# Last half's gates kept early in SBUF, its logits made from turned x2, its tile stores issued behind the logits

## The chip, the cores and the metric

The kernel runs on one core of one Trainium2 chip. The metric is device time in microseconds (us), the median of several executions. All data is fp32.

## The reference, cut to what matters

```
x = x + mamba(cond(x))            # D_INNER 512, 16 states, forward + reversed direction, in_proj/out_proj
x2 = x @ w_bot[b].T + bias        # per batch, 256 -> 256
# mixture of experts on x2, added to x2, the result added to x:
logits = x2 @ Wg + bg             # 256 -> 8
topv, topi = top_k(logits, 2);  w = softmax(topv)
xs = x2[:, :, None, :] * w[..., None]
out = x2
for e in range(8):
    h = silu(xs @ W1[e]) * (xs @ W3[e]);  y = h @ W2[e]
    out = out + where(topi == e, y, 0).sum(2)
result = x + out
# inside each direction of mamba:
x, z = split(h @ in_proj_w.T);  x = silu(conv(x));  ...;  y = scan(...) * silu(z)   # silu(z): the gates
return y @ out_proj_w.T
```

x is 2 batches of 1024 tokens by 256 channels. The gates multiply the sum of the forward and the reversed scan, since both directions share z.

## The kernel before, in words

The work has two big stages and a short one between them.

**The scan loop.** One program for each engine, each with the same loop over NU = 256 items. An item `i` is (q, th, pr, n): q is batch times direction (4 of them, 64 items each, `at(q, s)` is item 64q + s), th which half of the 512-token halves, pr which pair of the four 128-channel blocks, n the state. For an item ScalarE makes two decays (`decay`), VectorE does a product, two scans (`u`, `scans`) and, for every fourth item, one more product (`own_product`), GpSimd does the other products, and TensorE adds the result into two PSUM banks `Y[0]`, `Y[1]` by multiplying with the identity (`add`, two matmuls of 128x512). Sixteen items make one pair of blocks of one half; `evac` (ScalarE) then copies `Y` into `ya` in SBUF.

**Side work in the loop.** All else is hung on items by hand-written tables: `STEP_AT` (step widths; a matmul with 16 rows), `GATE_AT` (the gates z: two matmuls of 128x512, then Silu on ScalarE in place in PSUM, then `gated` on VectorE, the product with `ya`), `OUT_AT` (out projection, `out_block`), `TILE_AT` (a tile is 128 tokens: `tile` makes x2 and the turned x, `tile_T` turns x2 back to channels by tokens, `tile_lg` makes the logits, `tile_top` on VectorE takes the top two). TensorE runs a table's step in `side_work(i)` ahead of `add(i - 2)`; the other engines a few items later. Side work takes one of two PSUM banks (numbers 6 and 7, `both_side`); `take` waits until the bank's last user has freed it.

**Between the stages.** For the last half (batch 1, tokens 0 to 511, written (1, 0)) gates 0 and 1 stand at items 60 and 62 of q = 3, gates 2 and 3 after the loop; then `gated`, `out_block`, four `tile`, four `tile_T`, four `tile_lg`, one after the other on TensorE. The x2 and x rows of a tile are stored to DRAM by SyncE (`store`). VectorE then computes the routing: which of 39 (NT) tiles of 128 token slots belongs to which expert, in some 50 small steps that wait for each other by name (`after`, semaphore `dv_rt`): `mm` (the one-hot sum), a pair of 128x128 matmuls on it (L511, L512), `eid` (the expert of each tile), `hit`, `hot`. TensorE then multiplies 32 times 128x78 (L519, "the token lists" here) to invert the permutation. `warm(n)` is n matmuls of 128x512 into a bank that nobody reads, six behind `eid` and four behind the token lists.

**The expert stage.** 39 tiles: a gather of 128 tokens (GpSimd, `fetch`), W1, W3 and W2 of the expert loaded by SyncE (`load_13`, three buffers, 3 x 1 MB), matmuls L545 and L556, and an indirect DMA that adds to the output. The weights' buffers lie in the arena that the scan loop used.

## Time and profile before

| | us |
|---|---|
| median of 3 runs (1439.96, 1444.07, 1444.72) | 1444.07 |
| the profiled execution | 1444.52 |
| its span, first to last instruction | 1442.6 |
| scan loop, first scan to the last product of VectorE | 49.04 to 952.2 |
| between the stages, to the first expert matmul | 952.2 to 1010.91 |
| expert stage, 39 tiles | 1010.91 to 1442.6 |

All times below are from the span's start. A row of the timeline gives start, duration, engine, line, what is written from what, how many instructions, and in brackets the idle time before it and what ended it. An fp32 matmul is two instructions. Where rows of one engine overlap by some 0.1 us, the ends are modelled. The clock column gives TensorE's granted clock as a share of full speed: 1.00 is 2.4 GHz, 0.50 is 1.2 GHz.

### The profile page before, as it was taken

Reading aid. Unit: us, or ns where it says so; the run is one execution under the profiler, and the core shown is the slowest. Engines: PE = TensorE matmul, PEld = TensorE weight load, DVE = VectorE, ACT = ScalarE, POOL = GpSimd, SP = SyncE. Lnnn points to the kernel's source line nnn. Section 1 sums busy time; section 2 is a strip of 40 time slices with the busy share of each in tenths; the row PEclk is TensorE's granted clock in tenths of the full one; section 3 lists DMA queues with packets and bytes.
Section 4 is the critical chain, followed back from the end, with each engine's and each line's share of the span. In section 5 each row is a group of like instructions: output and inputs, shape, how many; then the busy total and the mean of one; then the engine's idle time right before and its main releaser. Section 6 shows DMA issues by size and latency. Waiting matters only on the chain.

```text
span 1442.6 us, 16563 instructions
## 1 busy us (share of the span) xinstructions
PE 1317.4 (91%) x5278; PEld 785.1 (54%) x5278; DVE 959.1 (66%) x1155; ACT 705.5 (49%) x1251; POOL 994.7 (69%) x519
## 2 busy tenths in 40 slices
PE   7999989899998978898888978897999999999997
PEld 3343333343333423333333434445999999999996
DVE  3798999999999999979999999955111111111110
ACT  3787775686786585766656564430211111111111
POOL 1799999999999999989999999931222222222211
PEclk9999999999998999979999999996999999999999
DMA  4645445445454445435554544514898898898892
GB/s 170 182 148 165 141 153 150 146 146 160 138 166 158 152 144 167 146 117 167 172 157 156 180 162 154 177 54 182 299 323 305 320 321 305 317 330 301 323 320 57
DMA packets 103193, 282.46 MB, mean 196 GB/s; under 512 B 9265, under 2 KB 19122, under 8 KB 87618
## 3 DMA queue, kind: packets, MB, share of 16 engines
q1 hardware_dynamic: 95618, 271.17, 54.6%
q0 software_dynamic: 7488, 10.23, 3.3%
q8 instruction: 43, 0.70, 0.2%
q14 instruction: 44, 0.36, 0.1%
HBM read 271.40 MB, written 9.96 MB: 195 GB/s over the span
## 4 chain that ended last, share of the span: by engine, by line
PE 32%; DMA 13%; POOL 5%; DVE 1%; SPq 1%; issue 1%; POOLq 0%; ACT 0%; DVEq 0%
DMA arena<-bc_scratch 12%; PE ps_y L545 10%; PE ps L556 9%; PE ps_du L545 5%; PE ps_u L545 5%; POOL arena L1083 3%; POOL arena L1079 1%; SPq L1169 1%; PE ps_de L519 1%; PE ps_de L531 1%; POOL arena L1051 0%; PE ps_y L414 0%; POOL arena L1069 0%; DMA out_x<-arena 0%; PE ps_du L361 0%
## 5 line engine op out<-in xcount | busy, mean ns | idle before, releaser
L414 PE MATMUL ps_y<-arena,ident 128*128 128x512 f32 x1024 | 510.2, 630 | 83.8 <-POOL arena L1083 82.6
L1083 POOL TENSOR_TENSOR arena<-arena 128x1024 f32<-128x1024 f32 x192 | 455.1, 2380 | 14.3 <-DVE arena L845 7.6
L414 PEld LDWEIGHTS ps_y<-arena,ident 128*128 128x128 f32 x1024 | 192.6, 197 | 364.0 <-issue 213.9
L658 ACT ACTIVATE ps_de<-arena,An 128x512 f32<-128x512 f32 x256 | 176.4, 689 | 264.6 <-DVE arena L842 263.7
L1069 POOL TENSOR_TENSOR arena<-arena 128x1024 f32<-128x1024 f32 x128 | 301.8, 2358 | 5.2 <-issue 3.6
L1121 POOL DMA_INDIRECT out_x<-arena x39 | 61.8, 1585 | 317.2 <-ACT arena L784 308.6
L829 DVE TENSOR_TENSOR ps_u<-ps_du,arena 128x512 f32<-128x512 f32 x256 | 178.6, 698 | 23.9 <-DVE arena L856 8.9
L658 ACT ACTIVATE arena<-arena,An 128x512 f32<-128x512 f32 x256 | 181.0, 707 | 0.0
L1034 DVE TENSOR_TENSOR arena<-ps_du,arena 128x512 f32<-128x512 f32 x39 | 27.0, 692 | 231.2 <-PE ps_du L545 231.2
L842 DVE TENSOR_TENSOR_SCAN arena<-ps_de,hlast,arena 128x512 f32<-128x512 f32 x128 | 163.0, 1274 | 0.3
L842 DVE TENSOR_TENSOR_SCAN arena<-ps_de,arena 128x512 f32<-128x512 f32 x128 | 155.3, 1213 | 4.8 <-ACT arena L658 2.4
L545 PE MATMUL ps_y<-arena 128*128 128x128 f32 x1248 | 152.1, 275 | 0.5 <-ACT arena L772 0.5
L545 PEld LDWEIGHTS ps_y<-arena 128*128 128x128 f32 x1248 | 148.4, 192 | 2.6 <-ACT arena L772 0.7
L556 PE MATMUL ps<-arena 128*128 128x256 f32 x624 | 141.2, 379 | 0.5 <-issue 0.5
L556 PEld LDWEIGHTS ps<-arena 128*128 128x128 f32 x624 | 115.6, 190 | 15.0 <-issue 0.9
L845 DVE TENSOR_TENSOR_SCAN arena<-arena,hlast,ps_u 128x512 f32<-128x512 f32 x96 | 120.5, 1255 | 0.0
L845 DVE TENSOR_TENSOR_SCAN arena<-arena,ps_u 128x512 f32<-128x512 f32 x96 | 114.6, 1194 | 0.0
L325 PE MATMUL ps<-arena 128*128 128x512 f32 x224 | 107.4, 602 | 0.0
L1034 DVE TENSOR_TENSOR arena<-ps_u,arena 128x512 f32<-128x512 f32 x39 | 27.0, 692 | 120.7 <-PE ps_u L545 120.7
L784 ACT ACTIVATE arena<-ps 128x256 f32<-128x256 f32 x39 | 14.9, 383 | 180.4 <-PE ps L556 171.1
L778 ACT ACTIVATE arena<-ps_y 128x512 f32<-128x512 f32 x78 | 46.6, 597 | 112.0 <-PE ps_y L545 112.0
L1079 POOL TENSOR_TENSOR arena<-arena 128x512 f32<-128x512 f32 x64 | 82.7, 1293 | 4.4 <-PE ps_y L414 4.4
(216 smaller groups left out, 1515.2 us busy)
## 6 DMA issues: line engine op xcount, KB each, us to landing
arena<-bc_scratch SPq DMA_DIRECT2D x256, 512.0 KB, 4.6
arena<-in_W SPq DMA_DIRECT2D x117, 1024.0 KB, 8.0
arena<-in_xT SPq DMA_DIRECT2D x2, 1024.0 KB, 5.5
arena<-in_w2c SPq DMA_DIRECT2D x1, 2048.0 KB, 8.3
arena<-in_xT SPq DMA_DIRECT2D x4, 512.0 KB, 6.2
X_scratch<-stg SPq DMA_DIRECT2D x12, 128.0 KB, 4.7
out_x<-stg SPq DMA_DIRECT2D x12, 128.0 KB, 4.9
ipT<-in_ipT SPq DMA_DIRECT2D x1, 1024.0 KB, 8.6
```

What stands on the lines that cost most here:

```text
L325: t = e.matmul(PS[p][:, :], cdiag[:, m % 2, k, :], xp[:, m, f:f + 512], start=(k == 0), stop=(k == KC - 1))
L414: t = e.matmul(Y[j][:, :], ident[:, :], hc[:, i % NP, j, :], start=False, stop=(n == 15))
L545: t = e.matmul(PS[o][:, j * 128:j * 128 + 128], w[:, i % NW, k, f:f + 128], xsT[:, i % 2, k, :], start=(k == 0), stop=(k == 1))
L556: t = e.matmul(PS[7][:, 0:C], hT[:, i % 2, k, :], w2[:, i % NW, k, :], start=(k == 0), stop=(k == 7))
L658: t = e.activation(DE[i % 2][:, :] if j else dA[:, i % ND, :], dt[:, width_at(q, th, m), :], ACT.Exp, scale=An[:, q % 2, m, n:n + 1])
L829: e.tensor_tensor(U[:, :], DU[:, :], ring[:, turn % NR, 0, i % 2, :], ALU.mult).then_inc(dv_u, 1)
L842: e.tensor_tensor_scan(hh[:, i % NH, 1, :], DE[i % 2][:, :], uA[:, i // 2 % 2, i % 2, :], hlast[:, 2 * pr + 1, n:n + 1] if th else 0.0, AL ...
L845: e.tensor_tensor_scan(U[:, :] if own(i) else hh[:, i % NH, 0, :], dA[:, i % ND, :], U[:, :], hlast[:, 2 * pr, n:n + 1] if th else 0.0, AL ...
L1069: e.tensor_tensor(uA[:, turn % 2, :, :], duA.rearrange("p (o t) -> p o t", o=1).to_broadcast([128, 2, TH]), ring[:, turn % NR, 0, :, :], A ...
L1079: e.tensor_tensor(hc[:, i % NP, 1, :], hh[:, i % NH, 1, :], ring[:, turn % NR, 1, i % 2, :], ALU.mult).then_inc(gp_hc, 1)
L1083: e.tensor_tensor(hc[:, i % NP, :, :], hh[:, i % NH, :, :], c, ALU.mult).then_inc(gp_hc, 1)
L1121: e.indirect_dma_start(out, bass.IndirectOffsetOnAxis(dest[:, i:i + 1], 0), yo[:, i % 3, :], None, compute_op=ALU.add).then_inc(l_add, 16)
```

## The change

1. **Gates.** The four gate matmuls of the last half move to items 57 and 61 of q = 2 and 6 and 10 of q = 3 (`LATE_AT`). ScalarE writes their Silu to SBUF (`zl`, the room of `xp`, which is dead by then) and frees the bank at once.
2. **No evacuation for the last half.** `last_gated` on VectorE multiplies the `Y` bank (read reversed) by `zl[m]` straight into `ya`: m = 0 and 1 behind item 50 of q = 3, m = 2 and 3 after the loop. The two `evac` of this half go.
3. **Out projection.** Its first two steps of four are hung on the last two items (TensorE's `side_work`), for output block 0 and block 1, in the side banks; the other two steps follow the loop.
4. **Logits.** Instead of four `tile`, `tile_T`, `tile_lg`: x2 turned (channels by tokens) is made for all 512 tokens by four matmuls of 128x512 with `wbot` as the weights, the bias is added by ScalarE and VectorE while they copy it to SBUF (`sTt`), and the logits come from it.
5. **Tiles behind the logits.** `last_x2(i)` makes x2 and x + x2 of one tile in one bank: two times (two matmuls of 128x256 and a bias matmul with one row), and x turned by multiplying with the identity. `last_x2(0)` stands ahead of L511 (now L539), the other three where `warm(6)` was. ScalarE copies the banks, SyncE stores them, all ahead of `load_13(0)`; `load_13(1)` waits until these stores have landed. `warm(6)` goes.
6. The wait for the stores moves from VectorE's first routing step to GpSimd, ahead of the first gather. Some items of `STEP_AT`, `GATE_AT`, `TILE_AT` and so on move by one to seven places. The original x of this half is loaded at item 55 of q = 3.

```diff
+LATE_AT = {at(2, 57): 0, at(2, 61): 1, at(3, 6): 2, at(3, 10): 3}
@@ out_block on TensorE
-                    is_free(("z", b, h, k))
+                    if (b, h) == (1, 0):
+                        e.wait_ge(dv_lg, k + 1)
+                    else:
+                        is_free(("z", b, h, k))
@@ side_work and the loop's end on TensorE
+                if i in LATE_AT:
+                    gate(1, 0, LATE_AT[i], side)
...
+                if i >= NU - 2:
+                    out_block(1, 0, i - NU + 2, side, (0, 1))
+
+            def last_x2(i):
+                cols = slice(i * 128, i * 128 + 128)
+                p = take(("x2", 1, i), [2, 3, 6, 7])
+                for w in range(2):
+                    at_w = slice(w * C, w * C + C)
+                    for k in range(2):
+                        e.matmul(PS[p][:, at_w], X[1][:, k, cols], wbot[:, 1, k, :], start=(k == 0), stop=False)
+                    e.matmul(PS[p][:, at_w], ones_r, bias2, start=False, stop=(w == 0))
+                for k in range(2):
+                    t = e.matmul(PS[p][:, C + k * 128:C + k * 128 + 128], X[1][:, k, cols], ident[:, :], start=False,
+                                 stop=(k == 1))
+                t.then_inc(full[p], 1)
...
-                else:
-                    e.wait_ge(dv_sA, i - 1)
-                    gate(*LAST_GATES[i - NU], [4 + i - NU])
...
+            for k in (2, 3):
+                for mo in range(2):
+                    out_block(1, 0, mo, both_side, (k,))
...
-            for i in range(4):
-                tile(1, i, every)
-            for i in range(4):
-                tile_T(1, i, every)
-            for i in range(4):
-                tile_lg(1, i)
...
+            last_x2(0)
@@ routing on TensorE
-            e.wait_ge(dv_rt, RT["eid"])
-            warm(6)
+            for i in range(1, 4):
+                last_x2(i)
+            for p in range(8):
+                e.wait_ge(freed[p], turns[p])
@@ VectorE
+            def last_gated(m):
+                e.wait_ge(pe_y, at(3, 32 + 16 * (m // 2) + 16))
+                is_read(e, ("z", 1, 0, m))
+                e.tensor_tensor(ya[:, m, HB[0]], Y[m % 2][:, ::-1], zl[m], ALU.mult).then_inc(dv_lg, 1)
...
+                if i == at(3, 50):
+                    for m in range(2):
+                        last_gated(m)
@@ SyncE
             for i in range(4):
-                store(1, i)
+                is_read(e, ("x2", 1, i))
+                for dst, w in ((X_dram, 0), (out, 1)):
+                    e.dma_start(dst[T + i * 128:T + i * 128 + 128, :], xc[0][:, i, w * C:w * C + C]).then_inc(l_st[2 + i], 16)
...
             for i in range(3):
+                if i == 1:
+                    for k in range(4):
+                        e.wait_ge(l_st[2 + k], 32)
                 if i == 2:
                     e.wait_ge(l_xi[0], 16)
                 load_13(i)
```

How the instructions move, at three places. `ps0` and `ps1` are the side banks, `ps_du` and `ps_u` two banks that only the scan loop used.

VectorE, item 50 of q = 3 (L829 is the next item's first product), before:

```order
L829 TENSOR_TENSOR ps_u<-ps_du,arena 128x512
L842 SCALAR_TENSOR_TENSOR arena<-ps_de0,hlast,arena 128x512
L845 SCALAR_TENSOR_TENSOR arena<-arena,hlast,ps_u 128x512
L875 TENSOR_TENSOR stg<-ps1,stg 128x256
L829 TENSOR_TENSOR ps_u<-ps_du,arena 128x512
```

and after:

```order
L862 TENSOR_TENSOR ps_u<-ps_du,arena 128x512
L875 SCALAR_TENSOR_TENSOR arena<-ps_de0,hlast,arena 128x512
L878 SCALAR_TENSOR_TENSOR arena<-arena,hlast,ps_u 128x512
L919 MAX mx<-ps0 128x8
L921 MAX_INDEX mi<-mx,ps0 128x8
L900 TENSOR_TENSOR arena<-ps_y0,arena 128x512
L900 TENSOR_TENSOR arena<-ps_y1,arena 128x512
L862 TENSOR_TENSOR ps_u<-ps_du,arena 128x512
```

Two products of the last half now stand in VectorE's loop (L900); before, none of this half did until the last item's work was over.

TensorE, the end of the loop, before (L351 is a gate, L414 an item's addition, L361 the out projection):

```order
L351 MATMUL ps_de0<-arena,ipT 128x512 x2
L414 MATMUL ps_y0<-arena,ident 128x512
L414 MATMUL ps_y1<-arena,ident 128x512
L351 MATMUL ps_de1<-arena,ipT 128x512 x2
L414 MATMUL ps_y0<-arena,ident 128x512
L414 MATMUL ps_y1<-arena,ident 128x512
L361 MATMUL ps_du<-arena,opT 128x512 x4
L361 MATMUL ps_u<-arena,opT 128x512 x4
L374 MATMUL ps_y0<-wbot,arena 128x256 x2
L375 MATMUL ps_y0<-arena 128x256
L377 MATMUL ps_y0<-ident,arena 128x128 x2
```

and after (L395, L396 are the logits of the last tile in the loop, L420 the addition, L364 the out projection):

```order
L395 MATMUL ps0<-wg,stg 128x8 x2
L396 MATMUL ps0<-arena 128x8
L364 MATMUL ps1<-arena,opT 128x512 x2
L420 MATMUL ps_y0<-arena,ident 128x512
L420 MATMUL ps_y1<-arena,ident 128x512
L364 MATMUL ps0<-arena,opT 128x512 x2
L420 MATMUL ps_y0<-arena,ident 128x512
L420 MATMUL ps_y1<-arena,ident 128x512
L420 MATMUL ps_y0<-arena,ident 128x512
L420 MATMUL ps_y1<-arena,ident 128x512
L420 MATMUL ps_y0<-arena,ident 128x512
L420 MATMUL ps_y1<-arena,ident 128x512
```

The gates are gone from the end, half of the out projection stands ahead of the last additions, and its second block takes `ps0`, the bank in which the logits just ahead of it were made.

TensorE, from the last logits to the token lists, before:

```order
L393 MATMUL ps_u<-arena 128x8
L511 MATMUL ps_y1<-arena,wmT 128x128
L512 MATMUL ps_y0<-arena,wmT 128x128
L505 MATMUL ps_de1<-opT,ident 128x512 x6
L519 MATMUL ps_de0<-arena 128x78 x32
L505 MATMUL ps_de1<-opT,ident 128x512 x4
```

and after:

```order
L528 MATMUL ps_y1<-arena 128x8
L495 MATMUL ps1<-wbot,arena 128x256 x2
L496 MATMUL ps1<-arena 128x256
L495 MATMUL ps1<-wbot,arena 128x256 x2
L496 MATMUL ps1<-arena 128x256
L498 MATMUL ps1<-ident,arena 128x128 x2
L539 MATMUL ps_y1<-arena,wmT 128x128
L540 MATMUL ps_y0<-arena,wmT 128x128
L495 MATMUL ps0<-wbot,arena 128x256 x2
L496 MATMUL ps0<-arena 128x256
L495 MATMUL ps0<-wbot,arena 128x256 x2
L496 MATMUL ps0<-arena 128x256
```

One `last_x2` (the first five rows behind the logits) now stands ahead of the pair that the routing waits for, and three of them in place of the six 128x512 matmuls L505.

## Rows read from the trace of the kernel before

**Rows 1.** Busy time by stage: stretch, length, each engine's busy time, clock, DMA share, GB/s.

```profile
800.00:952.00 152.00, 130.39 (x320) 57.53 (x321) 147.55 (x175) 81.03 (x137) 146.06 (x71) 0.96 0.47 155
...
1030.00:1200.00 170.00, 170.00 (x1297) 163.68 (x1296) 26.29 (x48) 30.98 (x63) 41.30 (x32) 1.00 0.89 317
```

**Rows 2.** Timeline, VectorE at the end of the loop.

```profile
950.19 1.26 DVE L845 TENSOR_TENSOR_SCAN ps_u<-arena,hlast,ps_u 128x512 f32<-128x512 f32 x1
...
952.10 1.27 DVE L862 TENSOR_TENSOR arena<-arena,ps 128x512 f32<-128x512 f32 x2
```

**Rows 3.** Chain of waits from the loop's end to the logits: start, length, what.

```profile
953.06 1.72 PE ps_de L351 x4
954.78 1.72 PE ps_y L414 x4
956.49 3.46 PE ps_du L361 x8
...
963.43 0.70 DVE arena L867
...
966.47 0.87 PE ps_y L374 x4
967.33 0.62 PE ps_y L375 x2
...
973.71 0.54 PE ps_de L392 x4
974.25 0.31 PE ps_de L393 x2
```

**Rows 4.** Timeline from the last logits to the token lists.

```profile
976.32 0.17 DVE L881 MAX8 mx<-ps_u 128x8 f32<-128x8 f32 x1 [0.40 <-PE ps_u L393]
978.58 0.77 PE L511 MATMUL ps_y<-arena,wmT 128*128 128x128 f32 x2 [2.30 <-DVE arena L950]
992.44 12.91 PE L519 MATMUL ps_de<-arena 128*128 128x78 f32 x64 [2.14 <-DVE arena L1009]
```

**Rows 5.** TensorE by stretch: stretch, length, busy, granted clock, DMA share, GB/s.

```profile
614.60:624.90 10.30, 10.30 (x12) 0.50 0.53 185
...
628.30:631.60 3.30, 3.30 (x9) 1.00 0.00 0
...
973.00:976.40 3.40, 3.28 (x24) 1.00 0.23 77
976.40:983.10 6.70, 1.19 (x4) 0.51 0.00 0
986.70:993.50 6.80, 4.66 (x19) 1.00 1.01 425
993.50:1003.80 10.30, 10.30 (x51) 0.50 0.70 291
```

**Rows 6.** Timeline, TensorE while the clock stayed at half.

```profile
616.89 2.07 PE L333 MATMUL ps<-arena,dtT 16*128 16x512 f32 x2
618.89 3.78 PE L414 MATMUL ps_y<-arena,ident 128*128 128x512 f32 x4
...
983.11 7.19 PE L505 MATMUL ps_de<-opT,ident 128*128 128x512 f32 x12 [3.35 <-DVE arena L978]
```

**Rows 7.** Timeline, SyncE's first weight loads and the first gather's end.

```profile
984.06 0.84 SPq L1211 DMA_DIRECT2D arena<-in_W  x2
1009.59 0.35 DVE L1027 TENSOR_SCALAR arena<-arena 128x256 f32<-128x256 f32 x1 [3.19 <-DMA arena<-X_scratch,arena]
```

**Rows 8.** DMA issues: kind, count, KB each, median us to landing.

```profile
X_scratch<-stg SPq DMA_DIRECT2D x12, 128.0 KB, 4.7
...
arena<-X_scratch,arena POOLq DMA_INDIRECT x39, 8.8
```

**Rows 9.** Waits of 700 to 952 us: engine, for whom, us, times, longest; and one table load.

```profile
ACT ps_de L658 <- DVE arena L842: 106.4, 59, 4.3
...
946.62 1.28 ACT L644 ACT_TABLE_LOAD   x1
```

More of the change, by code:

```diff
@@ L124, in build @@
         duA, uA = am.view(TH), am.view(2, 2, TH)
+        zl = [xp[:, m, 0:TH] for m in range(4)]
+        sTt = [xc[0][:, c, 2 * C:4 * C] for c in range(2)]
         dgw = hh.rearrange("p a j t -> p (a j t)")[:, 0:NB * E * 128].rearrange("p (k f) -> p k f", f=128)
@@ L751, in _ @@
                             gate(*GATE_AT[g])
+                if i - 2 in LATE_AT:
+                    gate(1, 0, LATE_AT[i - 2])
                 if i - 2 in TILE_AT:
@@ L755, in _ @@
                     tile_T(*TILE_AT[i - 4])
-            for m in range(1, 4):
-                gate(1, 0, m)
-            evac(NU - 1)
-            for i in range(4):
-                tile(1, i)
-            for i in range(4):
-                tile_T(1, i)
+            p = is_full(e, ("xT2", 0))
+            e.wait_ge(l_late, WL)
+            e.activation(sTt[0], PS[p][:, :], ACT.Identity, bias=b2c[:, 0:1]).then_inc(freed[p], 1)
             e.wait_ge(dv_rt, RT["ed"])
             e.activation(ed, ed, ACT.Exp).then_inc(ac_ex, 1)
+            for i in range(4):
+                p = is_full(e, ("x2", 1, i))
+                e.activation(xc[0][:, i, 0:2 * C], PS[p][:, :], ACT.Copy).then_inc(freed[p], 1)
             def xT(i):
@@ L1110, in _ @@
             e.wait_ge(dv_rt, RT["des"])
+            for k in range(2 + 4):
+                e.wait_ge(l_st[k], 32 * (6 if k < 2 else 1))
             def fetch(i):
```

86 lines of the change are left out of this document (51 added, 35 removed).

## The prediction

> **What bounds the kernel now.** I read busy time by stage first, then the chain of waits, then the timeline where the chain changes hands. In the last 152 us of the scan loop VectorE is busy 147.55 and GpSimd 146.06, and TensorE waits for them [rows 1]. In the expert stage TensorE is busy all of the time, at full clock [rows 1]; nothing there is touched. Between the stages the chain is nearly serial: the last additions and two gates on TensorE, the out projection, tiles, logits up to 976.3 [rows 3, 4], the routing's small steps on VectorE with a pair of matmuls at 978.58, the token lists from 992.44 to 1005.35 [rows 4], the first gather, the first expert matmul at 1010.91. What the change saves or costs is read at five marks: the last addition's end 956.49, the logits' end 976.3, the pair 978.58, the token lists' start 992.44 and their end 1005.35.
>
> **Mark 1, the last addition: 956.49 becomes 957.0 (+0.5).** VectorE bounds the loop's end, and it gets two products at item 50 of 0.64 each (two in 1.27 [rows 2]); before, the first of these products stood at 952.10, behind the last scan. So the last scans and products come 1.3 later, at 953.4 instead of 952.1. TensorE loses two gates of 1.72 between the last additions [rows 3] and gets two half out projections of 1.72 (half of 3.46 [rows 3]) ahead of them. The second one takes the bank of the last tile's logits, which VectorE frees only behind the scans of item 254. Those end one item's 3.15 ahead of item 255's (950.19 + 1.26 [rows 2]), at 948.3 before and 949.6 after, and its two small steps add 0.5. So TensorE starts it at 950.15, ends it at 951.9, and has three additions of 1.72 [rows 3] left: 957.0. Without that bank wait it would be 953.4 + 0.15 + 1.72 = 955.3. The four early gates cost nothing in the loop: on ScalarE one is two table loads of 1.28 and one Silu of about 0.6, 3.2 us, and ScalarE waited 106.4 us for VectorE in 59 pieces [rows 9]; if that cover is gone, one gate costs at most what it lacks, under 1 us each. The slots that move by a few items I take at zero, bounds -1 and +2: they are the same instructions on the same engines, and VectorE stays the one that is late.
>
> **Mark 2, the logits' end: 976.3 becomes 968.7 at full clock (-7.6).** Counted from the last addition's end X. The third gated product X + 0.75; then four half steps of 0.86 (a quarter of 3.46) to X + 4.25; VectorE's sum with x, 0.70 [rows 3], to X + 5.0. Of the turned x2, four matmuls of 0.86, the second two wait for the last sum at most: end X + 7.7. One copy with bias, 0.65, X + 8.4. Logits 4 x 0.85 (0.54 + 0.31 [rows 3]), X + 11.7. Before it was X + 19.8: 7.6 to the last sum's end, then four tiles, four turns and the same logits. So 957.0 + 11.7 = 968.7.
>
> **Mark 3, the pair: 978.58 becomes 975.6 (-3.0).** Here the gain shrinks twice. First, `last_x2(0)` stands ahead of the pair on TensorE, in order. By [rows 3] it is two times (0.87 + 0.62), and for x four instructions of 128 columns, each half of the 0.22 that one of 256 takes, with a start about 0.5: 3.5 us at full clock, and the routing's sum is ready after 1.7. Second, the clock. While TensorE made logits of 8 columns, busy 3.28 of 3.40 us by the record, the clock fell, and it stood at half through 976.4 to 983.1 [rows 5]. After the change these logits follow an idle wait of 0.7, so the same fall comes, somewhere between their first third and 1.2 us past their end. At half clock a matmul of 128x512 takes 1.72 and not 0.86, so `last_x2` goes to 4 x 0.86 for x2, 2 x 1.04 for the one-row matmuls (0.62 is 0.43 of streaming and 0.19 of waiting; twice 0.43, and 0.19) and 0.86 for x: 6.4 us. The logits themselves lose about 0.6 more. 968.7 + 0.6 + 6.3 = 975.6. Bounds: 972.3 if the clock didn't fall, 977.5 if it falls early.
>
> **Mark 4, the token lists' start: 992.44 becomes 996.5 (+4.1).** This is the term that decides. VectorE needs 13.86 us from the pair to the first `hot` and the start [rows 4], so TensorE has that much room for three `last_x2`. At full clock they take 10.5 and fit. At half clock they take 19.1: 975.6 + 1.1 (the pair) + 19.1 + 0.7 (ScalarE's last copy, which TensorE waits for) = 996.5. So does the clock come back? Before, the six matmuls of `warm(6)` did that: the clock rose while they ran back to back, all rows and 512 columns, and was 1.00 from 986.7 [rows 5, 6]. They are gone. `last_x2` is busy too, but of its 6.4 us at half clock 2.1 belong to matmuls with one row, in two pieces. The trace has two stretches in which TensorE was busy without a break and the clock stayed at half: 614.6 to 624.9, where matmuls of 16 rows stood between those of 128 rows, and 993.5 to 1003.8, the token lists with 78 columns [rows 5, 6]. In the first, 2.6 to 3.8 us of full matmuls at a time were not enough as long as a 16-row pair came in between; it rose once the full ones followed without a gap, 1.00 at 628.3 [rows 5]. The longest full piece in `last_x2` is x and the next x2, 0.86 + 1.72 = 2.6 us. That is nearer to the rows that stayed low, so I take the low clock. [...]
>
> **Marks 5 and 6.** The token lists at half clock from their first instruction: before, about 1.1 us of them ran at full speed; 51 instructions took 10.3 [rows 5], so all 64 take 13.5: end 1010.0 (+4.7). SyncE issues the last tile's stores only behind the last copy (996.5), then the first weights (before at 984.06 [rows 7], behind `eid`), and the second weights once the stores have landed, 4.7 later [rows 8], near 1002. Both loads together kept the DMA engines full from 985 through 993.5 and for 0.70 of the 10.3 us behind it [rows 5], some 16 us; so they are busy till about 1013, the first weights are there by 1006 in time, but the first gather, issued at 1011.3, meets the second. Alone it took 3.2 us [rows 7], among loads 8.8 [rows 8]; with 1 to 2 us of load left I take +1. Together 4.7 + 1.0 = +5.7. The expert stage then runs as before. The profiled execution was 1444.52, the median 1444.07: 1444.07 + 5.7 = 1449.8. GpSimd's moved wait for stores (landed near 1002) ends long before its gather at 1011 and costs nothing; if stores were late it would delay that gather alone.
>
> On the clock the Trainium skill, "TensorE: Matmul & The Clock Gate", section "The HAM clock gate", speaks against me: "The HW doesn't count instructions", it follows how busy the array has been, and sustained matmul activity lifts it. By that rule three busy `last_x2` would warm the clock as `warm(6)` did. The trace agrees on the fall and the rise [rows 5] but shows two busy stretches that did not lift it.
>
> **Rivals.**
> - *The clock comes back under `last_x2` (not slower).* For it: TensorE is never idle there, as under `warm(6)`; against it: rows 5 and 6. Then the three fit in VectorE's 13.9 us: the token lists start at 975.0 + 13.9 = 988.9 (-3.5). They end between 996 (full clock all through, half of 13.5) and 1002 (the clock falls again, as it did at 993.5 behind a 2 us wait). The gather doesn't profit: weights are then issued near 988 and 993 and fill the DMA till about 1005, so the gather lands near 1006.5 against 1009.6. The saving is 3 us, at most 4: 1441 (1439.5 to 1442.5). [...] Chance 0.36.
> - *The gain of the front arrives whole.* No bank wait at item 255 (-1.7), the clock falls late so that `last_x2(0)` costs 4 us (-1.5), and the first gather slips between the loads: 1437 to 1439. Chance 0.08.
> - *The loop pays.* The early gates stand near the step widths (16-row matmuls), where the profile has a stall of 6.8 us at half clock behind 614.6 to 624.9. If such a stall comes once more in q = 3, it adds 3 to 6 to either case: 1446 or 1454. Chance 0.08.
>
> **How the numbers follow.** Forecast, the clock stays low: 0.48, 1449.8, own range 1447.5 to 1452. The range 1439.5 to 1452.5 leaves out the whole gain (0.08) and the stall on top (0.05). Within 0.3% (about what a measurement here can tell) is 1439.7 to 1448.4: it holds most of the first rival (0.31), the low end of the forecast (0.05) and half of the stall. Faster: 0.08 and the rival's low end 0.05. Faster 0.13, same 0.40, slower 0.47. One run before was 1439.96, so that stall of the low clock may be absent in some runs, which blurs all cases by 4 us.
>
> **What would show it.** Mark 1: two L900 at item 50, and TensorE's second L364 starting behind VectorE's L921. Mark 3: the pair L539 behind `last_x2(0)`, more than 3 us behind its inputs. Mark 4: granted clock 0.50 from the logits through L549, and L495 at 0.43 an instruction; wrong if it is 1.00 there and VectorE's L1054 ends the wait. Mark 6: the gather slower than 3.2 us. The forecast fails as a whole if L549 starts before 992.4.

## The result, and the profile of the changed kernel

| | before | after |
|---|---|---|
| median, 20 runs each, us | 1442.82 (1431.78 to 1450.03) | 1445.49 (1441.61 to 1462.79) |
| ratio, after to before | | 1.0048, 95% interval 1.0028 to 1.0068 |
| the profiled execution | 1444.52 | 1441.82 |
| its span | 1442.6 | 1440.0 |

The changed kernel is slower by 0.48%, 6.9 us, with 4.0 to 9.8 in the interval (the plain means of the 20 runs, 1448.86 and 1442.68, are 6.2 apart). The medians are only 2.7 apart, since the runs of the changed kernel have a long upper end: 7 of its 20 lie above 1450, 1 of the 20 of before.

The profiled execution of after is one of its lowest, and even faster than that of before. So the two spans must not be compared as they stand. The stages show why. Up to item 52 of q = 2 nothing in the loop was moved, and still the profiled execution of after got there 8.3 us sooner (first scan of that item at 678.00 and 686.34). That difference comes and goes from one execution to the next: 4.7 of the 8.3 lie in items 0 to 52 of q = 2 (181.1 in after, 185.8 in before), and in the other profiled executions this stretch, with no edit in it, took between 181.0 and 185.7. Behind it:

| stretch, us | before | after |
|---|---|---|
| item 52 of q = 2 to the last item, first scans | 262.7 | 266.4 |
| last item's last scan to the first expert matmul | 60.7 | 61.3 |
| first expert matmul to the end | 431.7 | 433.1 |

That is +3.7, +0.6 and +1.4, together +5.7.

Timeline of after, the end of the loop, against [rows 2, 3]:

```profile
943.77 0.17 DVE L921 FIND_INDEX8 mi<-mx,ps 128x8 uint32<-128x8 f32 x1
943.99 1.98 PE L364 MATMUL ps<-arena,opT 128*128 128x512 f32 x4 [0.47 <-DVE mi L921]
...
945.63 1.26 DVE L878 TENSOR_TENSOR_SCAN ps_u<-arena,hlast,ps_u 128x512 f32<-128x512 f32 x1
945.81 5.31 PE L420 MATMUL ps_y<-arena,ident 128*128 128x512 f32 x12
...
951.16 1.29 DVE L900 TENSOR_TENSOR arena<-ps_y,arena 128x512 f32<-128x512 f32 x2 [3.54 <-PE ps_y L420]
```

The second half out projection starts right behind VectorE's top two (L921), and three additions stand behind it: the bank wait of the prediction. VectorE then waits 3.54 us for the last addition.

From the logits to the pair, against [rows 4]:

```profile
960.77 0.61 PE L527 MATMUL ps_de<-wg,arena 128*128 128x8 f32 x4
...
963.00 1.02 PE L527 MATMUL ps_y<-wg,arena 128*128 128x8 f32 x4
963.95 0.59 PE L528 MATMUL ps_y<-arena 1*128 1x8 f32 x2
964.47 2.08 PE L495 MATMUL ps<-wbot,arena 128*128 128x256 f32 x4
...
974.49 1.22 PE L496 MATMUL ps<-arena 1*128 1x256 f32 x2
```

Within the logits the same four instructions go from 0.61 to 1.02: the clock falls there. `last_x2(0)` (L495, L496, L498) then runs at half clock ahead of the pair, which starts at 971.79, 7.2 behind the logits' end; before it was 2.3.

TensorE by stretch in after, against [rows 5] (columns as there):

```profile
962.00:982.30 20.30, 20.30 (x53) 13.30 (x53) 11.71 (x50) 1.41 (x3) 1.56 (x1) 0.50 0.07 22
982.30:989.70 7.40, 6.46 (x28) 3.90 (x27) 6.48 (x4) 1.19 (x2) 1.99 (x1) 1.00 0.15 49
989.70:998.00 8.30, 8.29 (x67) 7.80 (x68) 0.84 (x6) 0.00 (x0) 0.00 (x0) 1.00 0.75 287
998.00:1002.70 4.70, 2.53 (x6) 0.76 (x4) 0.10 (x1) 0.00 (x0) 3.07 (x3) 1.00 1.02 431
1002.70:1009.60 6.90, 3.40 (x15) 3.00 (x16) 0.73 (x2) 1.67 (x2) 1.90 (x2) 0.51 1.01 372
1030.00:1200.00 170.00, 170.00 (x1287) 163.42 (x1286) 26.29 (x48) 30.67 (x63) 38.90 (x31) 1.00 0.90 317
```

TensorE was busy for all of 20.3 us and stood at half clock all that time; then the clock came back, under the second of the three `last_x2` behind the pair. The token lists ran at full clock, and it fell again at 1002.7 while TensorE waited for the first gather. The expert stage proper is as before.

From the last `last_x2` to the experts, against [rows 4, 7]:

```profile
988.80 0.60 ACT L799 ACTIVATE arena<-ps_u 128x512 f32<-128x512 f32 x1 [3.22 <-PE ps_u L498]
989.71 7.34 PE L549 MATMUL ps_de<-arena 128*128 128x78 f32 x64 [0.94 <-DVE arena L1054]
...
991.25 0.84 SPq L1260 DMA_DIRECT2D arena<-in_W  x2
993.48 0.84 SPq L1260 DMA_DIRECT2D arena<-in_W  x2
...
998.39 1.15 POOL L1162 DMA_INDIRECT arena<-X_scratch,arena  x1 [14.10 <-DVE arena L1066]
1005.32 0.35 DVE L1072 TENSOR_SCALAR arena<-arena 128x256 f32<-128x256 f32 x1 [7.22 <-DMA arena<-X_scratch,arena]
1005.73 0.69 PE L561 MATMUL ps_de<-ident,arena 128*128 128x128 f32 x2 [5.20 <-DVE arena L1072]
1006.89 3.30 PE L575 MATMUL ps_y<-arena 128*128 128x128 f32 x16 [0.47 <-ACT arena L805]
```

The lists (L549) take 7.34 where they took 12.91, 5.6 less. But the first gather, issued at 998.39, is read at 1005.32, 6.9 us later; before it was 2.9 on the same count (the row of [rows 7] has 3.19 of VectorE's wait, here 7.22). (L549 starts 0.3 behind the end of ScalarE's last copy, L799, which frees the bank; the four VectorE instructions that its row names were over at 988.78.) So the gather took 4.0 of the 5.6 that the lists gave. The first 8 expert matmuls (16 instructions) take 3.30, most of it at half clock; in the kernel before these took 2.05. From the second expert tile on, after keeps step with before, 1.3 to 1.4 behind.

### The profile page after: what moved, and what is told of

It reads as the page before. It is cut to its first block and busy times, and to the rows that moved or that the text cites. A ratio compares the mean times of both kernels' runs of the same rounds, so it can differ in the third digit from the quotient of the medians.

```text
span 1440.0 us, 16597 instructions
## 1 busy us (share of the span) xinstructions
PE 1316.0 (91%) x5298; PEld 787.5 (55%) x5298; DVE 959.9 (67%) x1152; ACT 709.5 (49%) x1248; POOL 994.8 (69%) x519
## 5 line engine op out<-in xcount | busy, mean ns | idle before, releaser
L420 PE MATMUL ps_y<-arena,ident 128*128 128x512 f32 x1024 | 508.7, 629 | 74.3 <-POOL arena L1128 73.2
L420 PEld LDWEIGHTS ps_y<-arena,ident 128*128 128x128 f32 x1024 | 194.5, 198 | 349.3 <-issue 217.9
L691 ACT ACTIVATE arena<-arena,An 128x512 f32<-128x512 f32 x256 | 181.0, 707 | 0.0
```

What stands on the lines that cost most here:

```text
L420: t = e.matmul(Y[j][:, :], ident[:, :], hc[:, i % NP, j, :], start=False, stop=(n == 15))
L691: t = e.activation(DE[i % 2][:, :] if j else dA[:, i % ND, :], dt[:, width_at(q, th, m), :], ACT.Exp, scale=An[:, q % 2, m, n:n + 1])
```

## The experiments

All times are against the kernel before, in interleaved runs: 12 of each experiment, and 29 to 35 of before beside them. The experiments ran in three groups: e0 to e3, e5 to e8, and e9 to e11, beside which the median of before was 1441.76, 1440.84 and 1440.76. Medians of different groups are best taken against these. Each kernel's profiled execution was read at the same marks. "Loop" is the stretch from item 52 of q = 2 to the last item; "front" is from the last scan to the first expert matmul; "low" is for how long the clock stood at half from the logits on, up to the lists; "gather" runs from its issue to VectorE's first read.

| kernel | median | ratio, 95% interval | loop | front | low | lists | gather | experts |
|---|---|---|---|---|---|---|---|---|
| before | | 1 | 262.7 | 60.7 | 10.5 | 12.9 | 2.9 | 431.7 |
| after | 1445.49 | 1.0048 [1.0028, 1.0068] | 266.4 | 61.3 | 20.3 | 7.3 | 6.9 | 433.1 |
| e0_after_again | 1445.18 | 1.0038 [1.0014, 1.0062] | 268.7 | 56.6 | 10.0 | 7.3 | 7.0 | 434.4 |
| e1_full_rows_bias | 1442.82 | 1.0013 [0.9995, 1.0031] | 268.9 | 57.1 | 7.0 | 13.9 | 3.0 | 431.8 |
| e2_pair_first | 1448.19 | 1.0047 [1.0026, 1.0067] | 268.3 | 59.1 | 13.5 | 7.3 | 6.9 | 434.5 |
| e3_gather_first | 1441.55 | 1.0016 [0.9984, 1.0047] | 268.8 | 52.4 | 10.5 | 7.3 | 3.1 | 433.9 |
| e5_old_slots | 1443.49 | 1.0023 [0.9999, 1.0046] | 269.1 | 61.0 | 24.0 | 7.3 | 6.1 | 433.8 |
| e6_evac_back | 1444.39 | 1.0034 [1.0015, 1.0053] | 266.0 | 56.1 | 7.0 | 7.3 | 7.0 | 434.3 |
| e7_rows_gather_warm | 1440.65 | 0.9992 [0.9971, 1.0013] | 269.1 | 50.5 | 7.0 | 7.3 | 2.9 | 434.1 |
| e8_before_warm8 | 1437.23 | 0.9978 [0.9956, 0.9999] | 262.6 | 55.1 | 10.0 | 7.3 | 2.9 | 432.0 |
| e9_front_and_evac | 1439.12 | 0.9979 [0.9963, 0.9995] | 265.6 | 51.4 | 6.5 | 7.3 | 2.9 | 435.5 |
| e10_gates_late | 1445.03 | 1.0022 [1.0003, 1.0042] | 271.9 | 51.4 | 7.0 | 7.3 | 2.9 | 436.0 |
| e11_gates_late_old_slots | 1436.21 | 0.9965 [0.9946, 0.9983] | 265.5 | 50.2 | 3.5 | 7.3 | 3.0 | 434.6 |

The stretches are of one profiled execution each, and the same program's can differ: the loop by 2.3 and the front by 4.7 between after and e0. The low stretch is read in steps of half a microsecond. The first four questions were about the front, the others about the loop.

### The changed kernel once more

No edit; it is the measure for the others.

> The changed kernel once more, to see a second execution and its spread. Theory (the clock falls at the 8-column logits and the x2 tiles, with their one-row bias matmuls, lift it late and by luck): from the last logits to the token lists 24 to 33 us, the granted clock 0.50 for 14 to 35 us, and the first gather 5 to 9 us; median 1443 to 1449, single runs up to 1462. Rival (the changed kernel is slower because of its loop): the loop's last quarter is more than 3 us longer than 221 us, and the stretch behind it is alike in all executions.

Measured: 1.0038. The front of this execution is 56.6, not 61.3, since the clock came back 10 us after its fall instead of 20. So one and the same program has fronts of two lengths. The loop is 268.7, 2.3 more than in the first profiled execution. The expectation missed in the front: the lists start 21.4 behind the last logits, not 24 to 33, and the clock was at half for 10, not 14 or more. The rival was half right: q = 3 up to its last item takes 224.7, more than 3 above 221, but the stretch behind it is not alike.

### Does the clock hang on the one-row matmuls?

```diff
-                    e.matmul(PS[p][:, at_w], ones_r, bias2, start=False, stop=(w == 0))
+                    e.matmul(PS[p][:, at_w], ident[:, :], b2f[:, :], start=False, stop=(w == 0))
```

`b2f` holds the bias in every row, so the result is the same, with 128 rows in place of one.

> One edit to the changed kernel: the bias of the last four tiles is added by a matmul of 128 rows (the identity times the bias in every partition) in place of one of one row. Same columns, same count, same order. Theory (one-row matmuls count little, so the clock stays low): the clock is back within 3.5 to 7 us of the first tile's first matmul, so at the latest during the second tile, the token lists never start later than 14.5 us behind the pair of 128x128 matmuls, and the runs above 1450 go; median 3 to 6 us below the changed kernel's. Rival (the clock comes back by time alone, whatever the rows): the low stretch is as long as in the changed kernel, 14 to 35 us, and the median moves less than 1.5 us.

Measured: 1.0013, median 2.4 below the changed kernel's on the same chip; the two intervals overlap, and 3 to 6 had been expected. No run of the 12 lies above 1447.7, where the changed kernel reached 1464.0. In its timeline TensorE gets back to full clock within `last_x2(0)`, ahead of the pair:

```profile
976.13 1.06 PE L497 MATMUL ps<-b2f,ident 128*128 128x256 f32 x2
976.98 1.91 PE L496 MATMUL ps<-wbot,arena 128*128 128x256 f32 x4
...
979.80 0.39 PE L540 MATMUL ps_y<-arena,wmT 128*128 128x128 f32 x2
980.02 0.39 PE L541 MATMUL ps_y<-arena,wmT 128*128 128x128 f32 x2
...
993.28 13.91 PE L550 MATMUL ps_de<-arena 128*128 128x78 f32 x64 [3.76 <-DVE arena L1055]
```

But now the three `last_x2` behind the pair are done 3.76 us before VectorE has the first `hot`, and behind that pause the lists run at half clock, 13.91. The gain of the warm front is lost again in the lists. Over all kernels of the study the low stretch was 10.0 to 24.0 in five of the six traces with one-row matmuls in `last_x2` and 7.0 in the sixth (e6_evac_back); in the five with full rows it was 3.5 to 7.0. Each is one execution, and e6 shows that one row doesn't always mean a long stretch. Of the runs, 19 of 80 lie above 1450 with one row, and 2 of 60 with full rows (both in e10_gates_late, whose loop is the longest). Four of the five kernels with full rows have other edits too; where the rows alone differ, it is 0 of 12 (e1) against 9 of 32 (after and e0).

### Is the pair better ahead of `last_x2(0)`?

```diff
-            last_x2(0)
...
-            for i in range(1, 4):
+            for i in range(4):
                 last_x2(i)
```

> One edit to the changed kernel: the first of the last four x2 tiles stands behind the pair of 128x128 matmuls and no longer ahead of it. Theory (the pair waits for the tile only): the pair starts 1.5 to 2.5 us behind the last logits instead of 7.3, but four tiles then stand ahead of the token lists, 14 us at full and 25.5 us at half clock, so the token lists start 16 to 27 us behind the last logits and the median moves by -2 to +1 us. Rival (the place ahead of the pair was the whole loss): the median is 5 us lower.

Measured: 1.0047, median 3.0 above e0_after_again, where -2 to +1 had been expected. The pair does start 1.8 behind the logits, not 7.2, yet the lists start later: 21.9 behind the pair. Its timeline:

```profile
976.54 0.80 PE L538 MATMUL ps_y<-arena,wmT 128*128 128x128 f32 x2 [1.81 <-DVE arena L992]
...
998.48 7.34 PE L548 MATMUL ps_de<-arena 128*128 128x78 f32 x64 [0.94 <-issue]
```

From the logits' end to the lists TensorE is the engine that everything waits for: four `last_x2` have to be done in either order, and an idle wait for the pair's inputs is added. The front is 59.1, between the 56.6 and 61.3 of the two executions with the late pair. So as long as TensorE bounds this stretch, the late pair, 3 us of the prediction, cost nothing that shows. Where VectorE bounds it, as in e1 (TensorE waits 3.76 ahead of the lists), an earlier pair could pay; no run tried it there.

### Is the gather held up by the second weights?

```diff
-                if i == 2:
+                if i:
                     e.wait_ge(l_xi[0], 16)
```

> One edit to the changed kernel: the second expert tile's weights are issued behind the first gather's end and not ahead of it. Theory (the gather meets these weights): the first gather takes 2.9 to 4 us and not 6.9, TensorE waits at most 5 us for it and the clock stays up, so the first expert matmuls take 2.05 us and not 3.3; median 2 to 5 us lower. Rival (the second tile's weights then come late): the second expert tile's matmuls wait for weights, and the median is the same or higher.

Measured: median 1441.55, 3.6 below e0_after_again; ratio 1.0016 with a wide interval that overlaps e0's, so the gain in time is not shown by the runs alone. The timeline is plain:

```profile
995.15 1.15 POOL L1162 DMA_INDIRECT arena<-X_scratch,arena  x1 [10.23 <-DVE arena L1066]
...
998.22 0.35 DVE L1072 TENSOR_SCALAR arena<-arena 128x256 f32<-128x256 f32 x1 [3.35 <-DMA arena<-X_scratch,arena]
999.01 0.81 SPq L1260 DMA_DIRECT2D arena<-in_W  x2
999.53 2.05 PE L575 MATMUL ps_y<-arena 128*128 128x128 f32 x16 [0.47 <-ACT arena L805]
...
1008.79 2.02 PE L575 MATMUL ps_y<-arena 128*128 128x128 f32 x16 [1.62 <-issue]
```

The gather takes 3.1 where it took 7.0, and the front is 4.2 shorter. In the five traces where the second weights were issued 4.9 us ahead of the gather it took 6.1 to 7.0, in all others 2.9 to 3.1 (in e1_full_rows_bias these weights had been issued 14 us ahead). Part of it is paid back: the second weights are issued at 999.01 only, and ahead of the second tile's matmuls TensorE stands still for 1.62. Counted from the first expert matmul, the third tile starts 1.9 later than in before, and no later tile falls back by more than another 0.2. In e7, e9, e10 and e11, which have this edit too, that lag is 2.1 to 3.9 by the third tile.

### Old slots

All tables as before the change, except `LATE_AT` and the load at item 55:

```diff
-           at(3, 11): (0, 0), at(3, 15): (0, 1), at(3, 19): (0, 2), at(3, 23): (0, 3),
+           at(3, 4): (0, 0), at(3, 12): (0, 1), at(3, 16): (0, 2), at(3, 20): (0, 3),
...
```

> The changed kernel with the item slots of the kernel before for step widths, the other half's gates, out projection and tiles; only the four early gates keep their new slots. Theory (the loop lost 4 to 6 us to where things now stand: gates beside logits and step widths, and two products in VectorE's loop): the stretch from item 52 of q = 2 to the last item is 262.7 us before and 266.4 to 268.9 after; with the old slots 264 to 267, the product pair and the early gates still costing 2 to 4 of it, and the bank wait ahead of the last additions is gone; median 1 to 3 us lower than the changed kernel's. Rival (the slots were moved for a reason and the old ones are worse with the early gates): 268 to 271, median higher.

Measured: 1.0023 (0.9999 to 1.0046); the loop is 269.1, no shorter, where 264 to 267 had been expected and the rival had 268 to 271. The bank wait ahead of the last additions is gone, as expected: the last addition ends 4.3 behind the last scan's start, not 5.5. What moved between items does change, item by item, but the sum stays:

| us from one first scan to the next | before | after | e0 | e5 | e6 | e10 | e11 |
|---|---|---|---|---|---|---|---|
| items 57 and 63 of q = 2 | 8.20 | 10.61 | 10.62 | 10.47 | 10.65 | 8.39 | 8.40 |
| items 2 and 3 of q = 3 | 8.36 | 7.11 | 7.10 | 7.08 | 7.11 | 8.51 | 8.36 |
| item 13 of q = 3 | 3.02 | 3.80 | 3.81 | 3.03 | 3.80 | 3.15 | 3.03 |
| items 17 and 30 of q = 3 | 8.61 | 6.17 | 6.39 | 8.60 | 6.45 | 6.45 | 8.62 |
| item 19 of q = 3 | 3.93 | 5.97 | 7.70 | 3.93 | 7.28 | 7.37 | 3.94 |
| items 50 and 51 of q = 3 | 7.26 | 8.74 | 10.44 | 11.53 | 7.28 | 10.70 | 8.36 |

Read by columns, e5 and e11 with the old slots, e10 and e11 without the early gates. The moved slots win 2.2 to 2.4 at items 17 and 30 and lose 2.0 to 3.8 at item 19. The early gates lose 2.3 to 2.8 at items 57 and 63 and win 1.3 back at items 2 and 3 of q = 3, in every kernel that has them. In e5 item 19 is back at 3.93, but item 51 is longer. The reason for item 57 stands in the timeline of after:

```profile
695.75 1.88 PE L351 MATMUL ps<-arena,ipT 128*128 128x512 f32 x4
...
697.90 0.39 PE L396 MATMUL ps<-arena 1*128 1x8 f32 x2
...
698.32 0.17 DVE L919 MAX8 mx<-ps 128x8 f32<-128x8 f32 x1 [1.06 <-PE ps L396]
```

The early gate L351 stands ahead of a tile's logits on TensorE, and VectorE, the engine that bounds the loop, waits 1.06 for those. At item 63 a gate's two table loads on ScalarE stand between the step widths' exponential and logarithm. And at item 19 of q = 3, without any gate, a tile and the logits of the tile before it come in one item on TensorE:

```profile
789.27 1.03 PE L377 MATMUL ps<-wbot,arena 128*128 128x256 f32 x4
...
791.57 0.38 PE L396 MATMUL ps<-arena 1*128 1x8 f32 x2
...
791.99 0.17 DVE L919 MAX8 mx<-ps 128x8 f32<-128x8 f32 x1 [1.83 <-PE ps L396]
```

That coincidence alone doesn't cost: in before, a tile and such logits stand together at items 16 and 20, and VectorE takes them without a wait (785.80 and 800.52). In after they stand right behind the first matmuls of a new pair of sums, which TensorE starts only when ScalarE has copied the last pair out (L411 at 785.73, behind L716) and ends at 789.27. No run moved this tile by itself.

### The evacuation and the products back

ScalarE's `evac` for the last half returns, the products of gates 0 and 1 stand behind the loop, and the whole out projection too:

```diff
-                if i >= NU - 2:
-                    out_block(1, 0, i - NU + 2, side, (0, 1))
...
-                if i == at(3, 50):
-                    for m in range(2):
-                        last_gated(m)
```

> The changed kernel with part 2 and 3 undone for blocks 0 and 1: ScalarE copies them out of PSUM inside the loop as before, VectorE multiplies them behind its last item, and the whole out projection follows the last addition. Theory (two products in the loop cost VectorE 1.3 us and make TensorE's additions wait for them, 0 to 1.7 more by the clock): items 50 and 51 of q = 3 take 7.3 us and not 8.7 to 10.4, the last addition ends 1 us sooner behind the last scan since no half projection stands ahead, and the logits come 2.4 us later behind the last addition; median -2 to +1. Rival (the products in the loop are hidden by GpSimd's and the DMA's waits): the loop is unchanged, median +1.5 to +2.5.

Measured: 1.0034; loop 266.0 against 268.7 (e0) and 266.4 (after), front 56.1 against 56.6. Items 50 and 51 are back at 7.28 (7.26 before). So the two products at item 50 cost 1.2, as predicted (1.3), and with item 51 1.5 to 3.2: TensorE's first additions of the next pair wait for them, and VectorE waits for TensorE an item later. In after:

```profile
901.29 1.27 DVE L900 TENSOR_TENSOR arena<-ps_y,arena 128x512 f32<-128x512 f32 x2
902.01 1.98 PE L411 MATMUL ps_y<-arena,diag 128*128 128x512 f32 x4 [1.87 <-DVE arena L900]
...
905.82 0.69 DVE L889 TENSOR_TENSOR arena<-ps_u,arena 128x512 f32<-128x512 f32 x1 [0.30 <-PE ps_y L420]
```

In e0 the clock fell in that place too, and item 51 took 5.95 in place of 4.25 (stretch of TensorE, columns as above):

```profile
909.00:915.10 6.10, 6.10 (x12) 2.48 (x11) 3.90 (x5) 1.33 (x2) 3.45 (x3) 0.72 0.70 235
```

For all that the front is not longer without them. Moving these products and half of the out projection into the loop bought nothing that shows, and the time is e0's within the intervals.

### The front's three faults mended

Full rows in the bias, the second weights behind the gather, and three matmuls of 128x512 ahead of the token lists, so that TensorE doesn't pause there:

```diff
             for p in range(8):
                 e.wait_ge(freed[p], turns[p])
+            warm(3)
             e.wait_ge(gp_rw, 1)
```

> The changed kernel with the bias matmuls of 128 rows, the second weights behind the first gather, and three matmuls of 128x512 into an unread bank ahead of the token lists. Theory: the clock is back during the tiles, stays up over VectorE's rest, the token lists take 7.4 us and not 14, the gather 3 us, so from the last scan to the first expert matmul 49 to 52 us in each execution (60.7 before, 56.6 and 61.3 after); median 1436 to 1439. Rival (the clock falls in the token lists themselves, since 78 columns are too few): they take 10 to 14 us and the median is 1440 or more.

Measured: 1440.65, ratio 0.9992, above the 1436 to 1439 expected; the median is 0.2 below before's beside it, where e0's was 3.4 above. The front is 50.5, 10.2 shorter than before; the lists take 7.34. Its timeline:

```profile
992.09 2.81 PE L534 MATMUL ps_de<-opT,ident 128*128 128x512 f32 x6 [0.94 <-issue]
...
994.92 7.34 PE L551 MATMUL ps_de<-arena 128*128 128x78 f32 x64
```

That the total is no better than before's puts the rest outside the front: loop +6.4, experts +2.4, of which 2.1 within the first two tiles.

### The kernel before with two more matmuls in `warm`

```diff
-            warm(6)
+            warm(8)
```

> The kernel before with eight matmuls of 128x512 ahead of the token lists and not six, so that TensorE idles under 0.7 us there and not 2.1. Theory (the token lists ran at half clock because of that pause): they take 7.4 us and not 12.9, the first gather is still at 2.9 to 3.5 us since both weight loads are through by then; median 2 to 5 us below the kernel before. Rival (78 columns are too few to hold the clock, whatever came ahead): 12 to 13 us as before, median within 1 us. It also gives a second look at the loop before: theory 262 to 264 us from item 52 of q = 2 to the last.

Measured: 0.9978 (0.9956 to 0.9999), median 3.6 below before's. Nothing of the change is in it. `warm(8)` reaches to the lists, which run at full clock (its timeline):

```profile
977.28 9.30 PE L505 MATMUL ps_de<-opT,ident 128*128 128x512 f32 x16 [3.34 <-DVE arena L978]
...
986.61 7.34 PE L519 MATMUL ps_de<-arena 128*128 128x78 f32 x64
```

So the 12.91 of [rows 4] came with TensorE's pause of 2.14 ahead of them, and filling the pause took 5.6 off. That saving could be had in the kernel before for one digit.

### The mended front with the loop's products back, and then the gates moved late

e9 is e7 with the edit of e6. e10 is e9 with

```diff
-LATE_AT = {at(2, 57): 0, at(2, 61): 1, at(3, 6): 2, at(3, 10): 3}
+LATE_AT = {at(3, 38): 0, at(3, 44): 1, at(3, 47): 2, at(3, 51): 3}
```

and e11 is e10 with all other tables as before the change, and the gates at items 37, 42, 45 and 49.

> Four edits of the earlier runs in one: the bias as a matmul of 128 rows, the second weights behind the first gather, three 128x512 matmuls ahead of the token lists (all as in e7_rows_gather_warm), and ScalarE's evacuation of the last half with the gated products behind the loop (as in e6_evac_back). If their effects add up, the loop's last stretch takes 266.0 (as in e6, against 269.1 in e7), from the last scan to the first expert matmul it is 50 to 51 (as in e7), and the time is 3 below e7's 1440.65: 1437.5, ratio 0.997. If instead the loop's stretch of 266 in e6 was chance, and all executions of these kernels stray between 266 and 269, it is 1440.5 again.

> The kernel e9_front_and_evac with the four gates of the last half at items 38, 44, 47 and 51 of q = 3, where no step widths are made, and no longer at 57 and 61 of q = 2 and 6 and 10 of q = 3. Theory: the early gates disturb the loop, at item 57 (they stand ahead of the logits that VectorE waits for) and at item 63 (their table loads fall between ScalarE's exponential and logarithm). Then items 52 to 63 of q = 2 take 41.7 as in the kernel before and not 44.0, items 0 to 31 of q = 3 no more than 112.5, and the time falls 2 to 3 below e9's: 1435. Rival: the gates are hidden and the moved slots of the other tables cost the time; then items 52 to 63 stay at 44.0 and the time is e9's within 1.

> The kernel e10_gates_late with all other tables at the places of the kernel before, and the gates at items 37, 42, 45 and 49 of q = 3 (between the tiles there). Theory (early gates are what cost): the loop's last stretch is 263 to 264, close to the 262.7 of before, and the time is e10's within 1, near 1434.5. Rival (the moved slots cost): 2 to 3 below e10, with items 52 to 63 of q = 2 back from 44.0 to 41.7 here and not in e10.

Measured: e9 0.9979 (0.9963 to 0.9995); the loop fell from 269.1 to 265.6, as in e6, so that effect adds up in the traces. The time doesn't follow in full: 1437.5 had been expected. The experts take 1.4 more than in e7, since TensorE waits 1.96 for the second tile's weights and the clock falls behind it.

e10 missed: 1.0022, and 5.9 above e9's median where 2 to 3 below had been expected. Items 52 to 63 of q = 2 are back at 41.8 from 44.0, as the theory had it (before: 41.7). Items 0 to 31 of q = 3 didn't get shorter without gates: 115.1 against 113.1 in e9 (at most 112.5 had been expected), with 1.4 of it at items 2 and 3. And at the new places the gates cost more than they did at the old ones, in this execution at least. Items 32 to 63 of q = 3 take 115.0 against 108.4 in e9; item 39 takes 6.84 (4.29 in e9) and item 50 takes 6.46 (3.29). Behind gate 2, at item 49, TensorE waits 4.82 for VectorE and its clock falls; one item's addition (four instructions) takes 3.62, where a later one takes 1.88, and at item 50 VectorE waits 3.05 for a tile's logits (timeline of e10):

```profile
911.09 0.66 PE L389 MATMUL ps<-ident,stg 128*128 128x128 f32 x2 [4.82 <-DVE stg L910]
...
911.54 3.62 PE L418 MATMUL ps_y<-arena,ident 128*128 128x512 f32 x4
...
920.10 0.17 DVE L916 MAX8 mx<-ps 128x8 f32<-128x8 f32 x1 [3.05 <-PE ps L397]
...
921.81 1.88 PE L418 MATMUL ps_y<-arena,ident 128*128 128x512 f32 x4
```

e11 is the best kernel of the study: 1436.21, ratio 0.9965 (0.9946 to 0.9983). Its loop is 265.5, with 41.9 at the end of q = 2, and its front 50.2, the shortest. I had asked 263 to 264 of that loop, and a time within 1 of e10's, which it beats by 8.8. The loop is 2.9 above before's 262.6 to 262.7, with the slots, the evacuation and the products all as before. Of these 2.9 only 1.6 lie in items 32 to 62 of q = 3, where the late gates are (1.3 at items 51 and 52, behind the gate at 49). The other 1.3 lie ahead of the first of them, 0.8 at item 31 alone, and there the loops of before and e8, which are the same program, differ by 0.7 too. So 1.6 is what can be put down to the gates at the best of the places tried, and 2.9 at most. Among the new slots of e10 the loop is 9.2 longer. The rival, that the moved slots alone make the loop's cost, falls with e5; that the early places alone make it falls with e10, whose loop is the longest without any early gate. Both are in it, and which of them meet decides. e11 undoes the moved slots and parts 2 and 3 of the change in large part; what is left of it is the late gates, the logits from turned x2 and the tiles behind them. Its interval (0.9946 to 0.9983) overlaps that of e8 (0.9956 to 0.9999), so it is not shown to beat the kernel before with `warm(8)`.

## Why the prediction was right, and where it was wrong

The direction was right, and the forecast of +5.7 lies in the interval of the measured +6.9; the median of after, 1445.49, is 4.3 below the 1449.8 given, and inside the range. But the sum came out of wrong parts, and that it came out is luck. Counted from the start of the last scan (951.46 by the prediction's own steps; 945.63 in after, 953.42 in e0):

| | predicted | after | e0 |
|---|---|---|---|
| last addition's end | 5.5 | 5.5 | 5.5 |
| logits' end | 17.2 | 18.9 | 18.0 |
| the pair | 24.1 | 26.2 | 25.2 |
| token lists' start | 45.0 | 44.1 | 39.4 |
| token lists' end | 58.5 | 51.4 | 46.7 |
| first expert matmul | 65.2 | 61.3 | 56.6 |

**Mark 1, the bank wait: right** to a tenth, in both traces. **Mark 1, the loop: wrong.** The loop was given +1.3 for the two products and nothing for the early gates and the moved slots. It costs +3.7 and +6.0: some 1.1 from the early gates (2.4 at items 57 and 63, less 1.3 at items 2 and 3), 0.4 and 2.3 from the slots at items 13, 17, 19 and 30, 1.5 and 3.2 at items 50 and 51, the rest (+0.7 and -0.6) in small pieces. The step that failed is "the four early gates cost nothing in the loop". It looked at ScalarE, where there was cover, and not at TensorE's order, where a gate stands ahead of logits that VectorE waits for (+1.2 at item 57), nor at ScalarE's order at item 63 (+1.2). e9 and e10 differ in the gates' places alone, and these 2.2 are gone in e10. The bounds given to the moved slots, -1 to +2, nearly held. The price of the products was right for their own 1.3 and left out who waits behind them.

**Mark 2: right**, 1.7 and 0.8 late, of which 0.6 was counted under mark 3. The clock fell inside the logits, as it was said to, and earlier than I took it: at 961.9, with half of the logits still to come.

**Mark 3: right** in mechanism, a little short in size: the pair starts 7.2 behind the logits' end, where 6.3 was forecast, since `last_x2(0)` takes 7.3 at half clock (964.47 to 971.79) and not 6.4. What I made of it was wrong: in e2 a pair ahead of `last_x2(0)` saved nothing, since TensorE was what the lists waited for.

**Mark 4: wrong**, and it was called the term that decides. The forecast held the clock at half through all three `last_x2`. It came back under the second of them in after (982.3) and earlier in e0, as in the first rival. That rival's own step, "then the three fit in VectorE's 13.9 us", was nearly right: the lists start 14.1 behind the pair in e0, bound by TensorE and ScalarE's last copy. In after, with 20.3 us at half clock, they start 17.9 behind it. What the forecast had seen is real, though: with one-row matmuls in between TensorE can be busy for 10 to 24 us and stay at half clock, with full rows it was 7.0 at most (e1 against e0, and the two groups behind it, which differ in other edits too). It is a matter of how long, and it differs between executions of one kernel, where I had made it a yes or no. I take the spread of the changed kernel's runs to be this, together with the loop; no trace of one of its runs above 1450 was taken, so that part is not shown. The runs' mean clocks say only this much: 0.953 on average in the 7 runs above 1450 against 0.965 in the other 13, by my estimate some 37 us more at half clock. That is more than the 14 us between the low stretches of e0 and e5 (10.0 and 24.0); in those runs the clock may have stayed low through the lists as well, as forecast, or have fallen more often in the loop.

On the clock's return, the Trainium skill, "TensorE: Matmul & The Clock Gate", section "The HAM clock gate", says that sustained matmul activity lifts the clock, and that the moment varies from run to run. The traces agree that it came back without `warm(6)`. They don't agree on the amount: the page gives about half a microsecond from run to run for its own case, and here the low stretch was 20.3 us in one execution and 10.0 in the other, with TensorE busy all through the 20.3.

**Mark 5, the lists: wrong**, by the same step. With the clock back, they took 7.34 and not 13.5. The rival had 7 to 13. (The 13.5 was also not what its own working gives: 51 instructions in 10.3 make 12.9 for 64. Lists that ran at half clock from the first instruction took 13.91, in e1.) **Mark 6, the gather: right in mechanism, mis-sized.** The collision with the second weights was named with +1.0; it is +4.0 (6.9 against 2.9; the 3.2 of the prediction is VectorE's wait). The main reason is mark 4 again: the forecast had 13.5 us of lists between the last copy and the gather, the trace has 7.3, so the gather was issued 4.9 behind the second weights (993.48) and not 9 behind them (1002), in the middle of 6 MB of loads. That the stores landed in 1.7 us and not in 4.7 worked the other way: it brought these weights forward, away from the gather. Here the first rival was right again: "the gather doesn't profit". e3 shows the size by taking it away. **The expert stage** was to be as before; it is +1.4 and +2.7, all but 0.3 of it in the first tile: the clock falls in the wait for the gather, and the first 16 instructions take 3.30 and 3.78 in place of 2.05.

So two errors of opposite sign met: the front was put at +4.5 by its own marks and came to +0.6 and -4.1; the loop and the experts were put at +1.3 and 0 and came to +3.7 and +1.4 (after), +6.0 and +2.7 (e0).

## What to carry to other kernels

Work that leaves a serial stretch must go somewhere: four gates, at 3.2 us of ScalarE and 1.7 of TensorE each, cost the bounding engine 1.6 to 2.9 us in the loop at the best places tried (e11), although each engine that runs them has room. At item 57 the trace shows why: it is what stands behind them in order. Check for each moved instruction who waits for the next one on its engine. And before a serial stretch is rebuilt, look at the pauses ahead of its longest dense pieces: two more matmuls in such a pause gave 0.22% here by themselves, where the change with its faults mended and its slots, evacuation and products put back gave 0.35%, and as it stood lost 0.48%.

## What the runs showed of the hardware that was not expected

- A pause of TensorE of 0.94 us ahead of the token lists left them at full clock (7.34 us, in eleven traces with this pause or none); pauses of 2.14 and 3.76 us ahead of them came with 12.91 and 13.91.
- TensorE was busy by the record for 20.3 us on end at half clock, in matmuls of 8 columns, of one row, and of 128 and 256 columns between them. With full rows in place of one, the clock was back within 7.0 us of its fall in five of five traces, and so it was in one of six with one row.
- A gather of 128 KB takes 2.9 to 3.1 us alone and 6.1 to 7.0 with weights of up to 6 MB issued 4.9 us ahead of it and before.
- The last tiles' stores of 128 KB landed in a median of 1.7 and 1.8 us in after, with the DMA engines 0.07 and 0.15 busy around them; in the loop of before the median was 4.7 [rows 8].

DMA issues of after, kind, count, KB, median us to landing:

```profile
out_x<-arena SPq DMA_DIRECT2D x5, 128.0 KB, 1.8
...
X_scratch<-arena SPq DMA_DIRECT2D x4, 128.0 KB, 1.7
```
